# The three products of probabilities and values of each group of heads, set next to one another in the order of the steps

## The reference

```
h = patches(x) @ W.T + b                      # 196 rows of 256 per image
h = concatenate([h, txt])                     # T = 324 rows
n = layernorm(h)
q, k, v = split into 16 heads of 16 (n @ Wq + bq, n @ Wk + bk, n @ Wv + bv)
att = softmax(causal(q @ k.T * 0.25))         # 324 x 324 for each head
h = h + merge(att @ v) @ Wo + bo
h = h + fp4_linear(silu(gate(layernorm(h))) * up(layernorm(h)))   # blockwise FP4, 704 wide
```

## Time and profile before

| | |
|---|---|
| runs | 2220.32, 2212.43, 2222.04 us; median 2220.32 |
| the profiled execution | 2218.99 us, its span 2217.2 us |
| PE busy | 1984.9 us (90%), 16096 matmuls |
| DVE busy | 1738.2 us (78%) |
| ACT busy | 1057.0 us (48%) |
| POOL busy | 980.8 us (44%) |
| L851, the attend products | 3072 instructions, 219.1 us busy, 366 ns each |
| L799 and L802, scores for the maxima | 1536 and 896 instructions, 265.6 and 215.8 us |
| L827 and L831, scores for the exponentials | 1536 and 896 instructions, 264.0 and 215.5 us |
| L532, the reductions | 448 instructions, 415.6 us, 928 ns each |
| L711, the exponentials | 512 instructions, 364.5 us, 712 ns each |

### The profile page before, as it was taken

One profiled execution on the slowest core, in us unless ns is written; L12 is line 12 of the kernel. 1 busy time (PEld: TensorE's weight loads), 2 busy tenths in 40 slices (PEclk: granted clock), 3 DMA queues, 4 the chain that ended last, 5 costly groups with the idle time before them and its releaser, 6 DMA issues. The chain is left out here.

```text
span 2217.2 us, 40958 instructions
## 1 busy us (share of the span) xinstructions
PE 1984.9 (90%) x16096; PEld 1580.4 (71%) x16096; DVE 1738.2 (78%) x3071; ACT 1057.0 (48%) x2075; POOL 980.8 (44%) x699
## 2 busy tenths in 40 slices
PE   3899999999999999999999848888888888888888
PEld 3687777777787777878777536666666666666666
DVE  5677777777777776676766349999999999999995
ACT  1355555555555554545454324444444444444443
POOL 6223232323232322232322016666666666666664
PEclk8899999999999999999999769999999999999997
DMA  5474747464656565565644021111111111111100
GB/s 117 70 96 82 95 82 95 82 93 84 91 87 91 86 87 90 78 99 77 100 66 67 14 62 34 36 37 36 36 37 37 40 39 36 36 36 36 36 30 29
DMA packets 129909, 142.02 MB, mean 64 GB/s; under 512 B 19894, under 2 KB 124854, under 8 KB 129718
## 3 DMA queue, kind: packets, MB, share of 16 engines
q1 hardware_dynamic: 122806, 138.40, 35.8%
q10 hardware_dynamic: 6912, 1.00, 0.3%
HBM read 51.25 MB, written 23.40 MB: 34 GB/s over the span
## 5 line engine op out<-in xcount | busy, mean ns | idle before, releaser
L532 DVE TENSOR_REDUCE maxima<-maxp 108x2 f32<-108x648 f32 (+2 forms) x448 | 415.6, 928 | 281.5 <-PE maxp L802 279.8
L711 ACT ACTIVATE probs<-expp 108x648 f32<-108x648 f32 (+2 forms) x512 | 364.5, 712 | 417.8 <-PE expp L831 401.3
L1115 POOL TENSOR_TENSOR q_b<-t_b,m_b 128x960 f32<-128x960 f32 (+2 forms) x85 | 192.5, 2265 | 272.0 <-DVE t_b L1177 272.0
L827 PE MATMUL expp<-qst,kst 99*108 99x324 bf16 (+2 forms) x1536 | 264.0, 264 | 25.5 <-ACT probs L711 12.3
L799 PE MATMUL maxp<-kst,qst 96*108 96x108 bf16 (+2 forms) x1536 | 265.6, 265 | 19.9 <-DMA kst<-parts 12.3
L451 POOL TENSOR_TENSOR rest<-qkf,parts 128x648 f32<-128x648 f32 x64 | 90.9, 1421 | 403.5 <-ACTq L684 403.5
L799 PEld LDWEIGHTS maxp<-kst,qst 96*108 96x108 bf16 x1536 | 163.8, 130 | 97.5 <-DVE maxima L532 48.4
L827 PEld LDWEIGHTS expp<-qst,kst 99*108 99x108 bf16 x1536 | 158.8, 130 | 92.2 <-ACT probs L711 33.8
L59 PE MATMUL gu<-wgu_hi,xqT 128*128 128x512 f32 (+1 forms) x486 | 215.8, 444 | 6.7 <-ACT xqT L1285 6.7
L851 PE MATMUL attp<-probs,vblk 108*32 108x324 f32 (+2 forms) x3072 | 219.1, 366 | 0.0
L802 PE MATMUL maxp<-mask_qk,identb 108*108 108x108 bf16 (+2 forms) x896 | 215.8, 247 | 0.0
(11 more groups left out here) (194 smaller groups left out, 5023.9 us busy)
## 6 DMA issues: line engine op xcount, KB each, us to landing
qst<-parts SPq DMA_DIRECT2D x192, 162.0 KB, 5.8
kst<-parts SPq DMA_DIRECT2D x192, 162.0 KB, 7.4
patches<-in_xT SPq DMA_DIRECT2D x32, 588.0 KB, 4.6
h_dram<-h_rows SPq DMA_DIRECT2D x32, 324.0 KB
xt<-h_dram SPq DMA_DIRECT2D x81, 128.0 KB, 2.3
res<-h_dram SPq DMA_DIRECT2D x81, 128.0 KB, 2.0
out_rows<-ot SPq DMA_DIRECT2D x81, 128.0 KB, 2.0
h<-in_txt SPq DMA_DIRECT2D x32, 108.0 KB
```

Source lines behind the costliest of these rows:

```text
L532: dve.tensor_reduce(rowmax[half][:, h:h + nh, c].rearrange("p (a h) -> p a h", a=2), src, AX.X, ALU.max).then_inc(maxp_free, 1)
L711: act.activation(dst, expp[0:CH, 0:banks, 0:per * w], ACT.Exp, scale=SCALE).then_inc(expp_free, 1)
L827: pe.matmul(expp[0:CH, a, x * w:(x + 1) * w], kst[s][0:ROWS + NPART, h, kc * CH:(kc + 1) * CH], qst[s][0:ROWS + NPART, h, kc * CH:T], star ...
```

## The change

It reorders the list. The three attend steps of each group stand next to one another: group 1's behind ("xnT", 1), group 2's between two tok steps, group 3's behind ("exp", 0, 0), group 0's behind ("exp", 1, 1). All other steps keep their order among themselves.

```diff
 STEPS = [
-    MAX_A[0], ("xnT", 0), ("xnT", 1), ("attend", 1, 0), ("exp", 2, 0), MAX_A[1], ("exp", 2, 1), ("tok", 1),
-    ("attend", 1, 1), MAX_A[2], ("w", 0), ("qk", 0), ("attend", 1, 2), MAX_A[3], ("exp", 2, 2), ("qk", 1),
-    MAX_A[4], ("exp", 2, 3), ("w", 1), ("qk", 2), MAX_A[5], ("w", 2), ("exp", 3, 0), ("attend", 2, 0),
-    ("tok", 1), ("w", 3), ("tok", 1), MAX_A[6], ("w", 4), ("exp", 3, 1), ("attend", 2, 1), ("attend", 2, 2),
+    MAX_A[0], ("xnT", 0), ("xnT", 1), ("attend", 1, 0), ("attend", 1, 1), ("attend", 1, 2), ("exp", 2, 0),
+    MAX_A[1], ("exp", 2, 1), ("tok", 1), MAX_A[2], ("w", 0), ("qk", 0), MAX_A[3], ("exp", 2, 2), ("qk", 1),
+    MAX_A[4], ("exp", 2, 3), ("w", 1), ("qk", 2), MAX_A[5], ("w", 2), ("exp", 3, 0), ("tok", 1),
+    ("attend", 2, 0), ("attend", 2, 1), ("attend", 2, 2), ("w", 3), ("tok", 1), MAX_A[6], ("w", 4), ("exp", 3, 1),
     ("w", 5), ("exp", 3, 2), ("neg", 0), ("qk", 3), ("tok", 1),
 ]
 
 STEPS += [
     MAX_B[0], ("exp", 3, 3), ("tok", 1), ("w", 6), ("tok", 2), MAX_B[1], ("tok", 2), ("part 1", 0),
-    ("exp", 0, 0), ("attend", 3, 0), MAX_B[2], ("tok", 1), ("exp", 0, 1), ("attend", 3, 1), MAX_B[3],
-    ("attend", 3, 2), ("exp", 0, 2), ("turn", 0), ("tok", 1), ("part 1", 1), ("turn", 1), ("tok", 1),
-    ("attend", 0, 0), ("h0",), ("exp", 0, 3), ("turn", 2), ("v", 0), ("w", 7), ("exp", 1, 0), MAX_B[4],
-    ("v", 1), ("exp", 1, 1), ("attend", 0, 1), ("xn",), MAX_B[5], ("turnback", 0), ("turnback", 1),
-    ("attend", 0, 2), MAX_B[6], ("w", 8), ("exp", 1, 2), ("v", 2), ("neg", 1), ("proj", 0), ("proj", 1),
-    ("exp", 1, 3), ("patches",),
+    ("exp", 0, 0), ("attend", 3, 0), ("attend", 3, 1), ("attend", 3, 2), MAX_B[2], ("tok", 1), ("exp", 0, 1),
+    MAX_B[3], ("exp", 0, 2), ("turn", 0), ("tok", 1), ("part 1", 1), ("turn", 1), ("tok", 1),
+    ("h0",), ("exp", 0, 3), ("turn", 2), ("v", 0), ("w", 7), ("exp", 1, 0), MAX_B[4],
+    ("v", 1), ("exp", 1, 1), ("attend", 0, 0), ("attend", 0, 1), ("attend", 0, 2), ("xn",), MAX_B[5],
+    ("turnback", 0), ("turnback", 1), MAX_B[6], ("w", 8), ("exp", 1, 2), ("v", 2), ("neg", 1), ("proj", 0),
+    ("proj", 1), ("exp", 1, 3), ("patches",),
 ]
```

## The result

The changed kernel takes 2249.49 us (median of 4 runs, 2248.17 to 2250.94), the kernel before 2217.27 us in the same series (4 runs, 2212.43 to 2222.04). The ratio is 1.0141, with a 95% interval of 1.0117 to 1.0164: slower by 32 us. The profiled execution of the changed kernel took 2248.17 us, 29 us more than that of before.

What follows compares the result with a forecast made beforehand. TensorE's queue order plus its waits was taken to bound the attention stage. Terms sum to 1.61 us an iteration, over some 30 iterations +48, less 3 = +45 on 2218.99: 2264 us, range 2244 to 2288.

Steps and rivals of the forecast that it cites:

- block of three: Three adjacent attend products on TensorE: 1.28 us (0.57 for chunk 0, 0.32 for chunk 2) against 1.50 apart.
- group 1, product 0 to max 2,0: 5.41 us becomes 5.53, +0.12: block's gain eaten by waits of 0.11 and 0.41 for VectorE's reductions.
- group 2, exp 3,0 to exp 3,2: 3.67 us becomes 4.37, +0.70: exp 3,2 still waits for ScalarE's exponential, now without two products as cover.
- group 3, product 0 to turn 0: +0.05 us: TensorE waits 0.59 at max 2,8; 0.13 taken off exp 0,2 to the turn.
- group 0, turn 0 to v 1: Stays 4.88 us, sum 0: VectorE's att releases v 1, so product 0's 0.77 us becomes a wait.
- group 0, v 1 to max 2,14: 3.31 us becomes 4.05, +0.74: the reduction still asks for about 1.5 us after product 2 goes.
- ScalarE's copies: Result copies (attT) move ahead of four steps on ScalarE: costed at nothing; uncovered, up to 0.4 us each.
- The cover ahead of the first exponentials: First exp of an iteration, waiting for the negated maxima's DMA, gets 0.6 us more cover: 3 us off in all.
- Waits hidden: Rival: reductions and exponentials release TensorE sooner, a half of 3.3 us waits vanishing decides it; 2165 us, chance 0.05.
- The block doesn't pack: Rival: a block takes 1.50 us in place of 1.28, +26 us, 2290 us; chance 0.10.
- Nothing to tell: Rival: missed slack takes the 1.6 us an iteration to below 0.37, giving 2219 to 2230 us; chance 0.05.
- The clock: Rival: new waits drop TensorE's granted clock; 2279 us if one in three does, 2309 if every one; chance 0.12.

Runs made afterwards that it cites:

- the short reductions: Changed kernel with VectorE's reduction of the maxima cut to the first 54 columns of each chunk: 2210.71 us, ratio 0.9962 to the kernel before.
- group 3 alone: Kernel before with only group 3's three products moved together, behind exp 0,0: 2216.06 us, ratio 0.9991.
- group 2 alone: Kernel before with only group 2's three products moved together, between the two tok steps: 2242.21 us, ratio 1.0093.
- the old order with short reductions: Kernel before, order kept, with VectorE's reduction of the maxima cut to the first 54 columns: 2209.41 us, ratio 0.9968.
- the order that uses both lessons: Kernel before with products joined only where no wait opens (groups 1, 2, 3) and w 1 moved behind max 2,4: 2190.58 us, ratio 0.9866.

## Why the prediction was right, point by point

The prediction was a loss of 45 us with a range of 2244 to 2288; 2249.5 lies in it, near its low end. The place of each loss was right, and each forecast was a little above what was measured.

| step of the prediction | forecast, us an iteration | measured (median of 27) |
|---|---|---|
| block of three | 1.28 | 1.23 |
| group 1, product 0 to max 2,0 | +0.12 | +0.03 |
| group 2, exp 3,0 to exp 3,2 | +0.70 | +0.60 |
| group 3, product 0 to turn 0 | +0.05 | -0.03 |
| group 0, turn 0 to v 1 | 0 | -0.02 |
| group 0, v 1 to max 2,14 | +0.74 | +0.70 |
| sum | +1.61 | +1.28 (whole iteration +1.32) |

*The price of the block.* 0.57 and 0.37 and 0.30 us (medians over the same iterations; the block's own row doesn't part them): product 0 saves the 0.11 carried over to it, product 1 saves more in the middle of a block than at its head (0.37 against 0.39), and product 2 saves 0.02, which the existing pair had hidden behind ScalarE. Four blocks, 0.2 us an iteration, 6 of the 15 us by which the forecast was high. The other terms of the sum make some 3 of them, and the cover below 5. That the pair's 0.11 would carry over to product 0 was a guess from one row, and it held.

*The waits.* The distances that the prediction called exact were: max 1,4 to max 2,0 is 640.42 - 638.50 = 1.92 us, max 1,12 to max 2,8 657.69 - 655.77 = 1.92, exp 3,1 to exp 3,2 648.62 - 647.28 = 1.34. TensorE's own idle time at them was 0.25, 0.41 and 0.80. In group 0, v 1 waited 0.83 for VectorE's att, and max 2,12 to max 2,14 took 1.51 for the 1.50 said. The waits of an iteration come to 2.6 us by their brackets for the 3.3 said, and the idle time of the middle stretch to 2.5; part of that difference is what the brackets leave out, as the short reductions show. ScalarE's copies were rightly priced at nothing: the exponentials behind them came no later (exp 2,0 to exp 2,1 1.38 us in both kernels, exp 3,1 to exp 3,2 1.34).

*The cover ahead of the first exponentials* seems worth more than the 3 us taken off. The irregular part of an iteration fell by 0.31 us in the mean, some 8 us over 27 iterations, of which 5 are the waits for the DMA themselves (7.0 to 2.1). The rest may be the clock, which fell behind such waits before: the granted clock of 1120 to 1200 us, 0.97 before, is 1.00 now. No run separates the two. And both figures come from one execution each, with a handful of such waits, which vary: in the kernels with the same single product ahead of exp 2,0 they come to 9.4 us (the kernel before), 7.6 (group 3 alone), 14.8 (group 2 alone) and 16.3 (the old order with short reductions). Product 0 ahead of exp 2,0 does count, as the 27.9 us without it show; what products 1 and 2 add there is not settled.

*Rivals.* "Waits hidden" didn't come: half of them would have had to vanish, and none did. The joins did pay: a block takes 1.23 us in place of 1.50, and TensorE's busy time fell by 45 us. By the Trainium skill (TensorEngine Tiling (Array Packing), Key Properties) a change of tiling mode drains TensorE. The trace agrees in that joined products are cheaper; that the drain is what they save, no run shows, and the rule says nothing of the wait behind it. "The block doesn't pack" is wrong by the table's first line. "Nothing to tell" is wrong by the result. "The clock" didn't come either:

```profile
640.00:720.00 80.00, 74.02 (x769) 63.80 (x768) 55.60 (x122) 42.00 (x73) 22.39 (x16) 1.00 0.54 84
```

TensorE is busy 74.0 of 80 us in place of 79.2, and the granted clock stays at 1.00.

## What to carry to other kernels

Where a buffer is single, a step that doesn't use it is cover for the engine that empties it; before moving it, measure the distance between the two uses and what the other engine needs, and if the two are equal, everything moved out comes back as a wait. A cheaper shape for the moved work (here joined products, 0.27 us a block) is worth having only where no wait opens that is longer than the gain, and every step between two uses of any single buffer counts, also at the place that it leaves.

## What the runs showed that I had not expected

VectorE's operation on 128 x 8 elements took 1.38 us beside a subtraction on GpSimd and 0.16 us without, and that delay came back as a wait of TensorE two steps later. It isn't a thing of one kernel: in the kernel before, 31 of the 33 executions of this operation start some 0.06 us behind that subtraction, take 1.38 us and end some 0.03 us behind its end; the two without it take 0.17 us. So the operation doesn't run slower, it ends when GpSimd's does. VectorE's reductions, whose input is in PSUM, aren't held up: in the order that uses both lessons those of max 2,4 take 0.83 us beside the same subtraction, as elsewhere. In the kernel before all this was hidden behind product 2,0 and what follows it. The Trainium skill (GPSIMD Engine Reference, Specifications) says that GpSimd's interfaces to SBUF are shared with VectorE and contend with some of its instructions, and the traces agree with it.

Moving this one step, with its neighbours unchanged, wasn't run by itself. But the stretch from exp 3,0 to exp 3,2 has the same order on TensorE in the two kernels with group 2's block between exp 3,1 and exp 3,2, and only w 1 ahead of it differs: it takes 3.59 us in the one and 3.22 in the other, some 0.37 us an iteration.
